# GpSimd without its wait for the edge matmuls: a graph layer's gathers, first edge loads and last two batches rearranged

## What is computed

```python
h   = maximum(layernorm(x), 0)
ea  = edge_attr @ W_edge.T + b_edge
msg = relu(h[src] + ea)
agg = segment_sum(msg, dst, 6250)
out = x + relu(((1 + eps) * h + agg) @ W1.T + b1) @ W2.T + b2
```

## Time and profile before

| what | value |
|---|---|
| time, median of 3 runs | 1250.83 us (1250.2 to 1250.99) |
| time of the profiled execution | 1253.34 us |
| its span in the profile | 1251.5 us |
| POOL busy | 787.0 us, 63% of the span |
| PE busy | 622.8 us, 50% |
| DVE, ACT busy | 517.4 us, 194.2 us |
| TensorE clock granted, mean | 0.60 of full speed |
| DMA | 93.30 MB, mean 75 GB/s |

### The profile page before, as it was taken

One profiled execution on the slowest core, in us unless ns is written; L12 is line 12 of the kernel. 1 busy time (PEld: TensorE's weight loads), 2 busy tenths in 40 slices (PEclk: granted clock), 3 DMA queues, 4 the chain that ended last, 5 costly groups with the idle time before them and its releaser, 6 DMA issues.

```text
span 1251.5 us, 9126 instructions
## 1 busy us (share of the span) xinstructions
PE 622.8 (50%) x2783; PEld 499.5 (40%) x2783; DVE 517.4 (41%) x659; ACT 194.2 (16%) x240; POOL 787.0 (63%) x838
## 2 busy tenths in 40 slices
PE   0544555454554555454544545554445444455538
PEld 0533444343443434343434434343334333344426
DVE  7853444443333334544333333344443333333542
ACT  5111111111111111111111111111111111111204
POOL 6666666666666666666666666666666666666620
PEclk9975556555555555655656556556655566555658
DMA  7522222222223222223222233222222222323202
GB/s 195 135 68 64 64 67 66 74 67 68 72 67 82 68 63 65 74 74 82 74 77 80 74 91 82 63 65 67 67 74 67 69 72 68 82 67 80 57 13 78
DMA packets 51183, 93.30 MB, mean 75 GB/s; under 512 B 17722, under 2 KB 20318, under 8 KB 51136
## 3 DMA queue, kind: packets, MB, share of 16 engines
q1 hardware_dynamic: 24390, 51.39, 14.6%
q0 software_dynamic: 26592, 40.85, 13.0%
q10 hardware_dynamic: 154, 0.48, 0.1%
HBM read 87.85 MB, written 4.80 MB: 74 GB/s over the span
## 4 chain that ended last, share of the span: by engine, by line
POOL 60%; issue 20%; another core or an unknown queue 13%; PE 2%; DVE 2%; DMA 1%; ACT 1%; DVEq 1%; SPq 0%; POOLq 0%; ACTq 0%
POOL gathered L345 60%; PE edge_ps L578 1%; DVE stats L616 1%; DMA h_table<-h_all 1%; ACT h_all L387 1%; PE agg_ps L563 1%; DMA x_all<-x_dram 0%; DVE edge_ps L803 0%; PE prep_ps L563 0%; PE const_ps L563 0%; DVEq L742 0%; DVE acc L733 0%; DVE edge_ps L820 0%; DMA gathered<-h_table,src_all 0%
## 5 line engine op out<-in xcount | busy, mean ns | idle before, releaser
L345 POOL DMA_INDIRECT gathered<-h_table,src_all x810 | 765.8, 945 | 394.8 <-issue 235.7
L450 PE MATMUL edge_ps<-w_edge,edge_in 97*128 97x96 f32 x1660 | 384.3, 415 | 530.5 <-DMA edge_in<-edge_t_dram 404.3
L450 PEld LDWEIGHTS edge_ps<-w_edge,edge_in 97*128 97x128 f32 x1660 | 348.6, 315 | 570.0 <-DMA edge_in<-edge_t_dram 421.6
L820 DVE TENSOR_TENSOR edge_ps<-edge_ps,gathered 128x960 f32<-128x960 f32 (+2 forms) x85 | 92.8, 1137 | 650.5 <-remote 647.8
L414 ACT ACTIVATE msg_parts<-edge_ps 128x960 bf16<-128x960 f32 (+2 forms) x85 | 80.7, 952 | 998.1 <-DVE edge_ps L820 994.4
L522 PE MATMUL agg_ps<-msg_parts,select 128*128 128x288 bf16 x826 | 185.1, 397 | 30.8 <-issue 30.6
L522 PEld LDWEIGHTS agg_ps<-msg_parts,select 128*128 128x128 bf16 x826 | 109.2, 134 | 105.5 <-issue 53.1
L692 DVE TENSOR_TENSOR select<-const_ps,dst_rel 128x2560 bf16<-128x2560 f32 (+3 forms) x45 | 123.1, 2738 | 29.5 <-issue 29.3
L803 DVE SCALAR_TENSOR_TENSOR edge_ps<-edge_ps,msg_parts 128x960 f32<-128x960 f32 (+2 forms) x85 | 92.8, 1138 | 1.9 <-ACT msg_parts L414 1.6
L830 DVE TENSOR_TENSOR msg_parts<-edge_ps,msg_parts 128x960 bf16<-128x960 f32 (+2 forms) x85 | 92.5, 1130 | 1.9 <-ACT msg_parts L419 1.6
L419 ACT CAST msg_parts<-edge_ps 128x960 bf16<-128x960 f32 (+2 forms) x85 | 79.7, 940 | 13.4 <-DVE edge_ps L803 8.7
(11 more groups left out here) (72 smaller groups left out, 128.9 us busy)
## 6 DMA issues: line engine op xcount, KB each, us to landing
edge_in<-edge_t_dram SPq DMA_DIRECT2D x165, 240.0 KB
gathered<-h_table,src_all POOLq DMA_INDIRECT x810
x_all<-x_dram SPq DMA_DIRECT2D x5, 420.0 KB
h_all<-x_dram SPq DMA_DIRECT2D x10, 210.0 KB
out_dram<-h_all SPq DMA_DIRECT2D x10, 210.0 KB
h_table<-h_all SPq DMA_DIRECT2D x4, 420.0 KB
dst_by_row<-dst_rows_dram SPq DMA_DIRECT2D x1, 480.0 KB
h_table<-h_all ACTq DMA_DIRECT2D x1, 420.0 KB
```

Of the source, the lines that this page charges most:

```text
L345: nc.gpsimd.indirect_dma_start(out=gathered[c % SLOTS][:, at:at + D], out_offset=None, in_=table, in_offset=bass.IndirectOffsetOnAxis(ap=s ...
L450: mm = pe.matmul(edge_bank(c, g)[:, (k - k0) * D:(k - k0 + 1) * D], edge_in[c % SLOTS][:, k * EDGE_TILE:(k + 1) * EDGE_TILE], w_edge[:], s ...
L820: last = nc.vector.tensor_tensor(in_banks(c, a, b), in_banks(c, a, b), in_rows(gathered[slot], a, b), ALU.add)
```

## The change

1. POOL no longer waits for `edge_half_done`, and the semaphore is gone. Only `added` (of batch c - 2, pair by pair) holds its gathers.
2. `h_all` is made and stored in five parts of 10, 10, 10, 5 and 15 columns: ACT makes the first four (35 columns), DVE the last (15). The two reductions of the destinations come later on DVE, among the work on the rows gathered for batch 0, and the bounds are made after the parts of batch 0 (`spread_bounds`). PE does the edges of batch 0 ahead of the spreading matmuls. The row of ones of `edge_in1` is copied by ACT, not set by DVE. SP loads the first edges only when the whole table is stored. POOL gathers 15 rather than 13 tiles of `x` ahead of its wait for the norm.
3. The last two batches are interleaved on DVE, PE sums batch 41 (`LATE`) before it turns the sums ahead, and batch 42 is summed in `edge_ps0` rather than in `agg_ps`.

```diff
-FIRST_BURST = 13
-ACT_CHUNKS = 4
+FIRST_BURST = 15
+TABLE_PARTS = ((0, 10), (10, 20), (20, 30), (30, 35), (35, 50))
+ACT_PARTS = 4
...
         def last_of(s):
-            return agg_ps[0:D, s * BANK:s * BANK + WINDOW]
+            return edge_ps[0][0:D, s * BANK:s * BANK + WINDOW]
...
+            sp.wait_ge(table_stored, 16 * len(spread) * len(TABLE_PARTS))
             load_edges(0)
...
             for c in range(1, BATCHES):
-                if c >= SLOTS:
-                    pool.wait_ge(edge_half_done, c)
                 for p, (k0, k1) in enumerate(pairs[c]):
...
+            act.wait_ge(ones_set, 1)
+            nc.scalar.copy(edge_in[1][D:D + 1, :], edge_in[0][D:D + 1, :]).then_inc(ones_copied, 1)
...
-                        if k == tiles_of[c] // 2:
-                            mm.then_inc(edge_half_done, 1)
...
-                    if c < LAST:
+                    if c < LATE:
                         pe.wait_ge(sums_made, this_window)
                         turn_sums()
-                        mm = sum_parts(c)
+                        sum_parts(c).then_inc(agg_done, 1)
+                    elif c < LAST:
+                        sum_parts(c).then_inc(late_summed, 1)
+                        pe.wait_ge(sums_made, this_window)
+                        turn_sums().then_inc(agg_done, 1)
                     else:
-                        mm = sum_last()
-                    mm.then_inc(agg_done, 1)
+                        sum_last().then_inc(agg_done, 1)
...
+            sum_windows(END, *end_bounds)
+            add_rows(LATE)
             add_turned()
-            sum_windows(LAST, *last_bounds)
+            take_high(LATE)
+            add_rows(LAST)
+            take_middle(LATE)
+            take_high(LAST)
+            take_middle(LAST)
+            sum_late_windows(*late_bounds)
+            sum_last_windows(*last_bounds)
```

More of the change, by code:

```diff
@@ L487, in _ @@
             selects = pe.alloc_register("pe_selects")
+            free = pe.alloc_register("pe_free")
+            pe.reg_mov(free, 1)
             def turn_sums():
@@ L752, in sum_windows @@
-                widest = max(tiles, tiles_of[ahead] + (ahead == LAST)) if step else tiles
+                step = first_tile[ahead] - at
+                widest = max(tiles, tiles_of[ahead] + (ahead == LAST))
                 with dve.Fori(0, span + 1, WINDOW) as done:
                     this_window = dve.snap(window)
-                    if c == LAST:
-                        for s in range(SIDES):
-                            next_node(s, firsts[s], done)
                     cols = [cols_of(s) for s in range(SIDES)]
-                    added_of = last_of if c == LAST else turned_of
@@ L777, in sum_windows, with sum_late_windows @@
                     make_select(c % 2, dve.snap(over, min_val=at, max_val=at + step), widest)
+                    dve.reg_add(window, window, 1)
+                    dve.reg_add(offsets, offsets, 1)
+            def sum_late_windows(firsts, span):
+                at, tiles = first_tile[LATE], tiles_of[LATE]
+                with dve.Fori(0, span + 1, WINDOW) as done:
+                    this_window = dve.snap(window)
+                    for s in range(SIDES):
+                        next_node(s, firsts[s], done)
+                    cols = [cols_of(s) for s in range(SIDES)]
+                    dve.wait_ge(late_summed, dve.snap(late))
+                    nc.vector.tensor_reduce(sums[:], parts_of(agg_ps), AX.X, ALU.add).then_inc(sums_made, 1)
+                    lower_offsets(at, tiles).then_inc(offsets_made, 1)
+                    dve.wait_ge(offsets_made, dve.snap(offsets) + 1)
+                    make_select(LATE % 2, at, tiles)
+                    dve.wait_ge(agg_done, this_window)
+                    dve.wait_ge(acc_summed, this_window)
+                    add_sums(0, cols[0], turned_of(0)).then_inc(side_summed, 1)
+                    dve.wait_ge(side_summed, this_window)
+                    add_sums(1, cols[1], turned_of(1)).then_inc(acc_summed, 1)
+                    dve.reg_add(late, late, 1)
+                    dve.reg_add(window, window, 1)
+                    dve.reg_add(offsets, offsets, 1)
@@ new lines, in sum_last_windows @@
+            def sum_last_windows(firsts, span):
+                at, tiles = first_tile[LAST], tiles_of[LAST] + 1
+                with dve.Fori(0, span + 1, WINDOW) as done:
+                    this_window = dve.snap(window)
+                    for s in range(SIDES):
+                        next_node(s, firsts[s], done)
+                    cols = [cols_of(s) for s in range(SIDES)]
+                    dve.wait_ge(agg_done, this_window)
+                    dve.wait_ge(acc_summed, this_window)
+                    add_sums(0, cols[0], last_of(0)).then_inc(side_summed, 1)
+                    lower_offsets(at, tiles).then_inc(offsets_made, 1)
+                    dve.wait_ge(side_summed, this_window)
+                    add_sums(1, cols[1], last_of(1)).then_inc(acc_summed, 1)
+                    dve.wait_ge(offsets_made, dve.snap(offsets) + 1)
+                    make_select(LAST % 2, at, tiles)
@@ L803, in rest_of, with add_rows @@
                 return nc.vector.scalar_tensor_tensor(message, message, 0.0, high, ALU.max, ALU.subtract)
[L805 removed]
+            def add_rows(c):
                 slot = c % SLOTS
[L807 to L813 removed]
                 dve.wait_ge(edge_done, c + 1)
@@ L829, in _ @@
                     for a, b in pieces(c, k0, k1):
-                        last = nc.vector.tensor_tensor(in_parts(parts, a, b, 2), in_banks(c, a, b), in_parts(parts, a, b, 1),
-                                                       ALU.subtract)
+                        last = nc.vector.tensor_tensor(in_parts(msg_parts[c % 2], a, b, 2), in_banks(c, a, b),
+                                                       in_parts(msg_parts[c % 2], a, b, 1), ALU.subtract)
                     last.then_inc(low_made, 1)
+            for c in range(LATE):
+                if c >= 1:
+                    bounds = load_bounds(c - 1)
+                add_rows(c)
+                take_high(c)
+                take_middle(c)
                 if c == TAIL_AT:
```

141 lines of the change are left out of this document (75 added, 66 removed).

## The result

The changed kernel takes **1295.3 us** (median of 4 runs, 1293.0 to 1297.0), the kernel before 1250.5 beside it: **ratio 1.036, 95% interval 1.034 to 1.037**. It is slower, where I had forecast 1233 as the likeliest. The time lies a microsecond above my whole range (1095 to 1294) and within rival C's (1281 to 1307).

A forecast was written before the change was run, and what follows sets the result against it. POOL with its pauses was taken as the path, its wait ended by a late half signal. 1253.3 - 15 (loop) + 2 (start) - 4.8 (end) - 2.5 (profile to median) = 1233 us, range 1095 to 1294.

The forecast's parts named there:

- rival C: Loop: PE's signals wait for POOL's bursts to end; period 29.4 to 30.1 us, total 1281 to 1307, chance 0.28.
- E: Loop: time from a batch's first edge matmul to its add; taken as 22.6 us, bounds 12.65 and 27.6.
- A: Likeliest case: the loop stays bound by the edge chain, period 28.3 us; 1233 us, range 1195 to 1250, chance 0.37.
- +18: Rival C's term at the start: batch 1's add comes up to 18 us later, without a pause before batch 2's burst.
- -10: Rival C's term near the end: batches 40 to 42 lose their half signals, about 10 us saved in all.
- A's -15 for the loop: Loop without POOL's wait: period 28.3 us, -0.4 us in each of 38 batches, -15 us.
- The half signal is in effect a whole one: Loop before the change: the half signal comes 12 us after its matmul's record, not before the full signal, so POOL waits.
- Rival B: Loop: POOL becomes the bound, E under 19.3 us, period 24.97; 1095 us, or 1100 without the start's gain, chance 0.22.
- The start: Table in five parts, two more gathers of x hidden: -4.2 us at best for the table; +2 in all, ends -5 and +6.
- The end: Last batches interleaved: two waits of about 2.65 us go, less 0.3 for switches; -4.8 us, ends -8 and 0.
- The skill's rule: Loop: if signals came as matmuls end, POOL's wait cost nothing and time would stay near 1246 us; the trace was said to disagree.
- rival D: Loop: a third thing, such as the gathers' queue, holds POOL and PE; period stays 28.72, total 1248 us, chance 0.13.

The follow-up runs named there:

- s5: Kernel before with probe signals on PE and, from batch 22 on, every second gather left out; 991.4 us beside 1251.0 for the kernel before.
- w2: Changed kernel with POOL's wait for the half signal put back; 1088.2 us, ratio 0.995 to the kernel before.
- s4: Kernel before with probe signals on PE and, from batch 22 on, every second gather left out; 876.9 us beside 1094.9 for the kernel before.
- q3: Changed kernel as it is, run again beside the kernel before; 1087.5 us, ratio 0.995.
- e4: Changed kernel with POOL's wait put back, its gathers also waiting until the previous batch's have landed; 1252.4 us, ratio 1.001 to the kernel before.
- w1: Kernel before with only POOL's wait for the half signal taken out; 1094.1 us, ratio 1.000.
- q2: Changed kernel with POOL's wait put back and probe signals on PE; 1089.0 us, ratio 0.996 to the kernel before.
- e3: Kernel before without POOL's wait, DVE's add from batch 1 on also waiting until the next batch's gathers have landed; 1297.8 us, ratio 1.039.

## Why the prediction was wrong

- **The step that failed is the size of E**: "I take 22.6, nearest to batch 40 (21.7) and the steady batches (23.02)". I took E for a length of PE's. It is the distance from the matmuls to POOL's last gather, plus some 3.4 us, and so moves with POOL: 23.9 in the changed kernel's loop, 27.5 us in its batch 0, 8.2 with half the gathers. The rows showed it: batch 19's and batch 40's signals 3.9 and 3.3 us behind the burst, which I wrote under C and did not follow, because batch 0's came in mid-burst. What made A the likeliest, "the loop's chain closes to the hundredth without POOL", was no evidence: from the first edge matmul of a batch to the add, and on to the first edge matmul of the next, is one period whatever bounds it. In the change batch 0's edges start 2.2 us behind POOL's first gather from the table (36.95) instead of two ahead of it, and it waits for the end too (66.63).
- **Rival C was the mechanism** in late sets, with a chance of 0.28. Its period, 29.4 to 30.1, was 29.6; its price of the first pair's add, 1.46, was 1.44; its total, 1281 to 1307, holds 1295. That the total fits is in part luck, since two of its terms were wrong and cancelled. +18 was for batch 1's add, which came 27 us later (96.20 for 69.03), but cost POOL nothing there (-0.1), since batch 2's burst hangs on batch 0's add. And -10 for batches 40 to 42 was +9.4, since POOL waits there for adds instead of half signals (2.8 us), and the adds, a batch further behind, have one more to make at the end (6.5).
- **A's -15 for the loop** was +35.3. "The half signal is in effect a whole one" was right (s5: 0.2 us apart), and so was "next in line is `added`": but I did not ask what restarts POOL there, an add that itself waits for POOL's silence.
- **Rival B was right for prompt chips**: period 24.97, 1087.5 against my 1095 to 1100. Only there the loop has 24.97 with the wait as well (w2, and s4 while it makes 20 gathers), so that nothing is gained by the wait's removal; POOL was the bound already.
- **The start**: the table 1.1 us earlier (prompt 3.2), under the 4.2 that I gave at best; the first edge matmul at 39.11, a microsecond before my 40 to 44. The 2.1 us between 1.1 and 3.2 are those by which DVE's wait for its own signal ended later (23.35 for 21.22), behind a burst of 15 rather than 13 gathers of `x`; q3, with the same 15, has no such wait. I had called the two gathers hidden. +2 in all was -0.1 in the change, 10 in e4. **The end**: -4.8 was -4.0 (the terms that I gave, twice 2.65 less 0.3, make 5.0).
- **The skill's rule**: by the Trainium skill ("TensorE: Matmul & The Clock Gate", the part on what overlaps and the one behind it on the semaphore tail) matmuls end in order and increment on completion. In the prompt sets the traces agree, to 0.01 to 0.04 us, and the wait does cost nothing there (w1: 1.000). The late traces don't: 12 us for the half signal. Of rival D so much held in every prompt set that only the start and the end count, for the reason that the rule gives; its third thing, which holds POOL and PE, showed in none.

**Which version to keep.** The change with the wait put back (w2, q2): 0.995 and 0.996 where signals are prompt, as good as the change itself, and 1.001 where they are late (e4, which has the hand-made wait too), against 1.039 for the kernel without it (e3, likewise). None that was run beats the kernel before in a late set.

## What to carry to other kernels

A wait that looks late for its purpose may be what keeps two engines in step, with a pause in which others' signals get through: before taking it out, ask what ends the wait that comes next, and whether that depends on the engine just set free. A length measured between two engines is nobody's own until something has changed it: look for the batch with another burst, another start, another count, and see which event it follows. And a time belongs to the chip and the occasion: compare only within one set of runs, and look at the signals' lag behind their matmuls before believing any reading of a trace.

## What the runs showed of the hardware

- The kernel before takes 1248 to 1251 us in three sets of runs and 1094 to 1096 in five others, its runs within a set lying within 0.4% of each other; one chip number gave both. In the late sets PE's signals come up to 15 us after the records of their matmuls while POOL issues indirect DMAs, and at 0.01 to 0.04 us in the prompt ones.
- It isn't PE's signals alone: in the late sets DVE waits 2.5 us (before), 5.4 (the change) and 4.7 (e4) for an increment of its own, behind POOL's first burst, and not at all in w1 and q3.
- POOL's gathers take 1.25 us each in both kinds; what differs is the pause between bursts: in the late sets 4.1 us after 20 gathers and 2.7 after 10 with POOL's wait in place (s5), 4.9 without it (the change), and none beyond the usual 0.3 us in the prompt sets.
- In the late sets PE's matmuls behind the edges really are slow late in a burst (0.7 to 2.1 us between the starts of single L539 matmuls of the change, 558.9 to 569.5 us). They are over when the edge signal is out (570.24), and so set nothing. What holds them is open.
